# A graph layer on one core: the first dense layer moved into the first gather, windows of 64 columns, and the selection of a turn built by two wide operations

## The reference, cut to what matters

```python
# 12500 nodes of 256 numbers, 212500 edges sorted by dst, all float32
xn = layernorm(x)
def gcn_layer(x, W, b):
    support = x @ W
    return segment_sum(support[src] * edge_weight[:, None], dst) + b
h  = elu(gcn_layer(xn, W1, b1))        # first layer
h  = elu(gcn_layer(h,  W2, b2))        # second layer
x  = x + h + linear_attention_and_mlp(xn)
x  = x + mixture_of_8_experts(layernorm(x))
```

## Time and profile before

| | us |
|---|---|
| median of three runs | 5660.61 |
| span of the profiled execution | 5671.8 |
| POOL busy | 3577.5 (63%) |
| PE busy / its weight loads | 4100.8 (72%) / 3754.5 (66%) |
| DVE busy | 2639.8 (47%) |
| ACT busy | 832.1 (15%) |

### The profile page before, as it was taken

How to read it: one execution, slowest core, us unless ns; L and a number is a source line. 1 busy time by engine, 2 the same in 40 slices (tenths; PEclk the granted TensorE clock), 3 DMA queues, 4 the chain that set the end, 5 groups by cost and what they waited for, 6 DMA issues and landing times. The chain is left out here.

```text
span 5671.8 us, 86295 instructions
## 1 busy us (share of the span) xinstructions
PE 4100.8 (72%) x25350; PEld 3754.5 (66%) x25351; DVE 2639.8 (47%) x8555; ACT 832.1 (15%) x2244; POOL 3577.5 (63%) x3748
## 2 busy tenths in 40 slices
PE   0566666666666666688888888888888777139998
PEld 0466666666656666588778778788787665138887
DVE  7433333333333323755555555555555588324444
ACT  2000000000000000611111111111111144001111
POOL 0677777777777777377777777777777522442222
PEclk9887888888888888899999999999999967569999
DMA  7444444444444444344444444444444366442221
GB/s 219 123 124 124 124 123 124 125 124 124 124 124 124 124 124 114 116 115 118 118 117 118 117 118 117 118 117 118 117 117 117 108 212 209 151 156 70 66 68 64
DMA packets 410309, 699.39 MB, mean 123 GB/s; under 512 B 103966, under 2 KB 276766, under 8 KB 410174
## 3 DMA queue, kind: packets, MB, share of 16 engines
q0 software_dynamic: 177584, 489.12, 30.6%
q1 hardware_dynamic: 196773, 168.65, 9.9%
q10 hardware_dynamic: 35920, 41.25, 2.1%
HBM read 565.09 MB, written 133.62 MB: 123 GB/s over the span
## 5 line engine op out<-in xcount | busy, mean ns | idle before, releaser
L374 PE MATMUL sums<-sel,rows 128*128 128x128 f32 x13312 | 1997.5, 315 | 1037.0 <-DMA rows<-xn,idx 430.3
L374 PEld LDWEIGHTS sums<-sel,rows 128*128 128x128 f32 x13312 | 1910.1, 228 | 1139.0 <-issue 776.3
L421 POOL DMA_INDIRECT rows<-xn,idx x1664 | 1591.3, 956 | 642.5 <-issue 632.8
L421 POOL DMA_INDIRECT rows<-h,idx x1664 | 1590.2, 956 | 529.0 <-issue 511.7
L390 DVE TENSOR_TENSOR agg<-agg,sums 128x256 f32 x416 | 175.6, 422 | 1554.1 <-PE sums L374 1554.1
L384 DVE TENSOR_SCALAR sel<-cols,rel_now,wgt_now 128x128 f32<-128x128 f32 x3344 | 891.4, 364 | 8.0
L1705 PE MATMUL y_ps<-w,e_hidden 128*128 128x256 f32 x1248 | 287.3, 390 | 0.0
L1693 PE MATMUL e_hidden_ps<-tokens_t,w 128*128 128x256 f32 x1248 | 279.9, 382 | 4.9 <-DVE e_hidden L1762 4.0
L1705 PEld LDWEIGHTS y_ps<-w,e_hidden 128*128 128x128 f32 x1248 | 242.8, 197 | 33.6
L1633 POOL DMA_INDIRECT out<-y_result,target_i x80 | 79.8, 998 | 293.5 <-DVE y_result L1747 273.5
L1693 PEld LDWEIGHTS e_hidden_ps<-tokens_t,w 128*128 128x128 f32 x1248 | 237.8, 191 | 40.8 <-DVE e_hidden L1762 7.3
(11 more groups left out here) (205 smaller groups left out, 4874.1 us busy)
## 6 DMA issues: line engine op xcount, KB each, us to landing
xe<-zeros ACTq DMA_DIRECT2D x104, 258.0 KB, 3.8
rows<-xn,idx POOLq DMA_INDIRECT x1664
rows<-h,idx POOLq DMA_INDIRECT x1664
w<-in_ffn_w POOLq DMA_DIRECT2D x16, 1024.0 KB
tile<-xn SPq DMA_DIRECT2D x105, 128.0 KB
ln_rows<-in_x SPq DMA_DIRECT2D x52, 256.0 KB
xn<-ln_normed ACTq DMA_DIRECT2D x52, 256.0 KB, 4.3
kv_tile<-xn SPq DMA_DIRECT2D x104, 128.0 KB
```

What stands on the lines that cost most here:

```text
L374: last = nc.tensor.matmul(sums[g][:, h, :], rows[:, u, k, h * P:(h + 1) * P], sel[:, k, :], start=(c == 0), stop=(c == GROUP - 1))
L421: nc.gpsimd.indirect_dma_start(out=rows[:, u, k, :], out_offset=None, in_=source, in_offset=bass.IndirectOffsetOnAxis(ap=idx[:, u, k:k + 1 ...
```

## The change

Gather stages: a turn keeps its 16 slots but has 4 groups of 4 slots; a window has 64 nodes; two groups share a PSUM bank. `sel` and `rel_now` get two halves. The selection of a whole turn (16 slots by 64 columns, 1024 elements per partition) is built by two tensor-tensor operations one turn ahead, in place of 16 with two per-partition scalars each. PE takes the groups in order; DVE adds four windows, each behind the one before; PE's first product of a turn waits for `turn_added`. The places of the attention's pieces in a turn stay.

First dense layer: units of 128 nodes; the unit of turn t-8 is done in turn t of gather 1 (copy and exp on ACT, product on PE between the two banks, bias, max and elu on DVE, store on SP). After the last turn units 96 and 97 remain. Should a group's first node lie below what was already taken, all units are done again at the end; this is worked out in prepare. The stage of its own is gone, and POOL has no part in the layer. The loops of gather 1 have 6 double turns written out ahead of the loop, where before it was one.

```diff
-GROUP = 8
-TURN = 2
+GROUP = 4
+TURN = 4
+SUB = 2
+BANKS = TURN // SUB
-WIN = 128
+WIN = 64
+LAG = 8
+UNITS = 2 * -(-N // (2 * P))
...
-        def selection(g):
-            for c in range(GROUP):
-                k = g * GROUP + c
-                last = nc.vector.tensor_scalar(sel[:, k, :], m.cols[:, :], rel_now[:, k:k + 1], wgt_now[:, k:k + 1],
-                                               ALU.is_equal, ALU.mult)
-            return last
+        def of_window(of):
+            return of.rearrange("p (c o) -> p c o", o=1).to_broadcast([P, SLOTS, WIN])
+        def same_node(u):
+            return nc.vector.tensor_tensor(sel[:, u, :, :], m.cols[:, :].rearrange("p (o w) -> p o w", o=1)
+                                           .to_broadcast([P, SLOTS, WIN]), of_window(rel_now[:, u, :]), ALU.is_equal)
+        def weigh(u, t):
+            return nc.vector.tensor_tensor(sel[:, u, :, :], sel[:, u, :, :],
+                                           of_window(m.wgt[:, bass.ds(t * SLOTS, SLOTS)]), ALU.mult)
...
                 def turn(i, u):
                     t = 2 * i + u
+                    dense.dve(dve, i, u, 0)
                     mix.dve(dve, i, u, 0)
-                    selection(1).then_inc(sel_ready[1], 1)
+                    if not before_first(i, u, 1):
+                        dve.wait_ge(summed[BANKS - 1], t)
+                    take(t + 1, 1 - u)
                     mix.dve(dve, i, u, 1)
...
-                    add_window(0, low[0]).then_inc(added, 1)
-                    mix.dve(dve, i, u, 2)
...
+                    for g in range(TURN):
+                        if g % SUB == 0:
+                            if g:
+                                mix.dve(dve, i, u, 2)
+                                dense.dve(dve, i, u, 1)
+                            wait_apart(dve, summed[g // SUB], t + 1, m.passed)
+                        if g or not before_first(i, u, 1):
+                            dve.wait_ge(added, t * TURN + g)
+                        add_window(g, low[g]).then_inc(added, 1)
...
-                    take(t + 1)
+                    dve.sem_inc(turn_added, 1)
                     mix.dve(dve, i, u, 3)
...
+    def product(pe, j, u):
+        pe.wait_ge(nodes_ready, 2 * j + (u + 1))
+        for k in range(KD):
+            last = nc.tensor.matmul(z, nodes[:, k, :], w_g1[:, k, :], start=(k == 0), stop=(k == KD - 1))
+    def elu(dve, j, u, fresh):
...
+        nc.vector.tensor_scalar(positive[:, :], pre[:, :], 0.0, -1.0, ALU.max, ALU.add).then_inc(positive_ready, 1)
...
+        nc.vector.scalar_tensor_tensor(h[:, u, :], exps[:, :], 1.0, positive[:, :], ALU.min, ALU.add
+                                       ).then_inc(h_ready, 1)
+    def act(act, i, u, place, turn_added):
+        if due(i, u):
+            if place == 0:
+                act.wait_ge(turn_added, 2 * i + u)
+                copy_nodes(act, i - behind, u, 2 * (i - behind) + u)
+            if place == 1:
+                exponential(act, i - behind, u)
+    def act_end(act, turn_added):
+        act.wait_ge(turn_added, TURNS)
+        for n in range(TURNS - LAG, UNITS):
+            copy_nodes(act, n // 2, n % 2, n)
+            exponential(act, n // 2, n % 2)
...
-            gather(nc, m, 1, m.xn, keys_values)
-            dense_first(nc, m)
-            gather(nc, m, 2, m.h1, attend)
+            gather(nc, m, 1, m.xn, keys_values, dense_first)
+            gather(nc, m, 2, m.h1, attend, apart)
```

More of the change, by code:

```diff
@@ L134, in prepare @@
         span = sb("span", [TURNS, TURN], I32)
-        more = sb("more", [TURNS, 1], I32)
+        more = sb("more", [TURNS, 2], I32)
+        least = sb("least", [TURNS, 1], I32)
+        taken = sb("taken", [TURNS, 1], I32)
         dst_i = sb("dst_i", [P, NCH], I32)
@@ L263, in _ @@
                 dve.wait_ge(step, 4)
-                nc.vector.tensor_reduce(more[:, :], high[:, :], AX.X, ALU.max).then_inc(spans_done, 1)
-                stat_steps = 5
+                nc.vector.tensor_reduce(more[:, 0:1], high[:, :], AX.X, ALU.max).then_inc(step, 1)
+                nc.vector.tensor_reduce(least[:, :], low[:, :], AX.X, ALU.min).then_inc(step, 1)
+                wait_apart(dve, taken_ready, 1, m.passed)
+                dve.wait_ge(step, 6)
+                nc.vector.tensor_tensor(more[:, 1:2], least[:, :], taken[:, :], ALU.is_lt).then_inc(spans_done, 1)
+                stat_steps = 7
                 def statistics(i, s):
@@ L365, in gather, with window_products @@
         further_step = sem("further_step")
+        further_steps = 2 + TURN
         mix = mixer(nc, m, sb, sem, ps)
+        dense = denser(nc, m, sb, sem, ps)
         loops = TURNS // 2
-        def window_products(g, h, u, before):
-            for c in range(GROUP):
-                k = g * GROUP + c
[L374 to L377, removed]
-            return last
-        def selection(g):
-            for c in range(GROUP):
-                k = g * GROUP + c
-                last = nc.vector.tensor_scalar(sel[:, k, :], m.cols[:, :], rel_now[:, k:k + 1], wgt_now[:, k:k + 1],
-                                               ALU.is_equal, ALU.mult)
-            return last
+        def window_products(b, s, u, before):
+            for h in range(KD):
+                for c in range(GROUP):
+                    k = (b * SUB + s) * GROUP + c
+                    last = nc.tensor.matmul(sums[b][:, s, h, :], rows[:, u, k, h * P:(h + 1) * P], sel[:, u, k, :],
+                                            start=(c == 0), stop=(c == GROUP - 1))
+                    if h == 0 and c == 0 and before is not None:
+                        last.then_inc(before, 1)
+            return last
+        def of_window(of):
[6 more added lines that the diff above has]
+                                           of_window(m.wgt[:, bass.ds(t * SLOTS, SLOTS)]), ALU.mult)
         def add_window(g, at):
             window = m.agg[:, :, bass.ds(at, WIN)]
-            return nc.vector.tensor_tensor(window, window, sums[g][:, :, :], ALU.add)
+            return nc.vector.tensor_tensor(window, window, sums[g // SUB][:, g % SUB, :, :], ALU.add)
         with nc.Block(f"gather{layer}") as block:
@@ L398, in _, with turn @@
                 mix.load_weights(sp)
-                with sp.Fori(1, loops) as i:
-                    for u in range(2):
[L402 to L407, removed]
+                dense.load_weights(sp)
+                def turn(i, u):
+                    sp.wait_ge(rows_loaded[u][BANKS - 1], 16 * GROUP * SUB * i)
+                    sp.dma_start(idx[:, u, :], m.in_src[bass.ds(2 * i + u, 1)].rearrange("o p c -> (o p) c")
+                                 ).then_inc(idx_loaded[u], 16)
+                    mix.free(sp, i - 1, u)
+                    mix.load(sp, 2 * i + u, u)
+                    mix.store(sp, i - 1, u)
+                    dense.sp(sp, i - 1, u)
+                for i in range(1, dense.peeled):
+                    for u in range(2):
+                        turn(i, u)
+                with sp.Fori(dense.peeled, loops) as i:
+                    for u in range(2):
+                        turn(i, u)
+                for u in range(2):
+                    dense.sp(sp, loops - 1, u)
                 mix.load_past(sp)
                 mix.stored(sp)
+                dense.sp_end(sp)
                 sp.wait_ge(m.xe_zeroed, 16 * TURNS)
@@ L516, in _, with apart @@
-                two_by_two(pe, loops, turn)
+                    mix.pe(pe, i, u, TURN)
+                two_by_two(pe, loops, turn, dense.peeled)
                 mix.pe_end(pe)
+                dense.pe_end(pe)
         mix.after()
+def apart(nc, m, sb, sem, ps):
+    dense = Memory()
+    dense.peeled = 1
+    dense.load_weights = dense.sp_end = dense.dve_begin = dense.dve_end = lambda engine: None
+    dense.pe_end = dense.pe_begin = lambda engine: None
+    dense.sp = dense.pe = lambda engine, i, u: None
+    dense.dve = lambda engine, i, u, place: None
+    dense.act = lambda engine, i, u, place, turn_added: None
+    dense.act_end = lambda engine, turn_added: None
+    return dense
```

341 lines of the change are left out of this document (187 added, 154 removed).

## The result

The changed kernel takes 5682.15 us (median of 5 runs, 5681.56 to 5695.59), the kernel before 5663.88 us beside it (5 runs, 5658.44 to 5666.25). The ratio is 1.0038, with a 95% interval of 1.0025 to 1.0051: slower, by 18 us in the medians. The profiled execution took 5681.56 us.

A forecast was written before the change was run, and what follows sets the result against it. POOL's indirect DMA strings were taken to bound the kernel. The removed stage's -90 us and +95 us, mainly from wide operations stopping POOL, gave +5 on the 5660.6 us median: 5666 us, range 5620 to 5715 (8 in 10: 5590 to 5745).

The forecast's parts named there:

- The bound: Both gathers: POOL's unbroken strings of 1664 indirect DMAs set the time, 20.2 us a turn; PE and DVE keep pace.
- The stage between the gathers: Between POOL's two strings: 122.4 us without row fetches shrinks, gaining 93 us, taken as 90.
- The 3 us taken off: Off the stage's gain: first products wait for both wide operations (2.5 us); gather 2's last products may run at lower clock.
- The first wide operation: Selection in both gathers: stops POOL's DMA until it ends, 0.46 us a turn in the mean at equal chance.
- The Trainium skill's rule taken whole: Shared SBUF port: a two-SBUF-input operation holds POOL for all 1.23 us; 0.60 us a turn, some 25 us slower than forecast.
- The second wide operation: Selection in both gathers: ends 1.26 us after the first, adding 0.03 us a turn to POOL's stops.
- The old selection's share: Both gathers: the removed narrow selection's part in POOL's longer DMAs, 10 us back.
- The min-and-add: Elu of the dense layer moved under POOL: two SBUF inputs also stop POOL, 3 us.
- Narrower windows: PE's window products: 64 columns take the same time as 128, nothing gained, nothing lost.
- Wide operations that seldom stop POOL: Rival, both gathers: wide operations cost POOL only 0 to 0.15 us a turn; about 5580 us; chance 0.13.
- A stop of nearly the whole length: Rival, each turn of both gathers: wide operations stop POOL 1.0 us a turn, 208 us; 5771 us; chance 0.09.
- PE as the bound: Rival, gather 1: low clock makes PE's turn 21.6 us against 20.2, 150 us more; 5768 us; chance 0.08.

The follow-up runs named there:

- E1: Changed kernel with the two wide selection operations replaced by 16 narrow ones a turn: 5571.61 us, ratio 0.9828 to the kernel before.
- E3: Changed kernel with a third wide operation right behind the two in gather 2, into a spare tile: 5689.84 us, ratio 1.0031 to the kernel before.
- E7: Changed kernel with a third wide operation by itself in gather 2, between the adds of the two banks: 5727.06 us, ratio 1.0118.
- E2: Changed kernel with node numbers and weights copied to PSUM in gather 1 alone, wide operations kept, gather 2 as control: 5635.08 us, ratio 0.9937.
- E5: Narrow windows alone: changed kernel with 16 narrow selection operations and the dense layer back between the gathers: 5654.20 us, ratio 0.9986.
- E6: Changed kernel with each wide operation cut into 8 pieces in gather 1 and 4 in gather 2: 5598.62 us, ratio 0.9892.

## Why the prediction came out as it did

**The bound** was right: POOL's string sets both gathers before and after, and E1 shows that all else that moved fits under it.

**The stage between the gathers**: -91.8 us where the steps gave -93, less 3. The steps hold one by one: the last bank's products began 3.6 us after POOL's last DMA (forecast 3.7), the two units took 3.3 us each (forecast 3.5). The gap came to 30.6 us where the steps gave 29.1. The 3 us taken off rested in part on the wrong reason. E1 and E3 both have a shorter gap, 26.2 and 27.1 us, and E3 keeps the wide operations. What differs is PE's clock at the end: the changed kernel's 16 last products, then E1's and E3's:

```profile
2320.56 3.52 PE L380 MATMUL sums<-sel,rows 128*128 128x64 f32 x16
```
```profile
2260.46 1.90 PE L380 MATMUL sums<-sel,rows 128*128 128x64 f32 x16
2321.53 1.90 PE L381 MATMUL sums<-sel,rows 128*128 128x64 f32 x16
```

The granted clock over the last 32 products of gather 1's windows was 0.52 in the changed kernel's profile, 1.00 in E1's and E3's. The forecast had priced the low clock, and in this profile it was granted; at the high one the gap would have been some 3 us shorter.

**The first wide operation**: 98.1 us over 208 turns, 0.47 each, where equal chance gave 0.46. The mechanism held, but that the size came so close was partly luck. The moments aren't spread evenly: of the 201 in L390, 56 lie 0.30 to 0.45 us into it and none in the next 0.15. And the first operation's loss in a single gather 2 went from 0.35 us a turn (E7) over 0.40 (E3) to 0.54 (E2). What sets the place against POOL's beat stays open. The unheld first 0.15 us, taken from two rows, held in all 27 cases. The Trainium skill's rule taken whole (SBUF — State Buffer, "Who interferes with whom") made it 0.60; E2 bears out its condition, two SBUF inputs, and the trace its length only without that start.

**The second wide operation** is the term that was mis-sized: 0.03 us a turn expected, 0.084 measured, 17.4 us in place of 6. I had its end follow the first's by 1.26 us; it waits for the first's result and starts 1.35 us after it, 0.09 behind POOL's beat of 1.255.

**The old selection's share** was put at 10 us, read as 11.1. **The min-and-add** was put at 3, read as 2.1. **Narrower windows** were put at nothing. For the time that held as far as E5 tells; the 9 us less stretch there lie in narrow operations of selection, which the changed kernel doesn't have. For PE it didn't hold: its clock fell.

**Sum.** -91.8 + 98.1 + 17.4 - 11.1 + 2.1 = +14.7, for +5 forecast; 11 of the difference are the second operation. The medians differ by 18 us, the two profiled spans by 8. The profile before was taken of an execution whose span lay 11 us over the median, the changed kernel's of one within 2 us of it. The undisturbed DMA took 949 ns in the first and 946 in the second, 10 us over 3328, and such a step also shows between E1 (946) and E2 (949) on one chip. No run tells where it comes from.

**The rivals.** Wide operations that seldom stop POOL would have given means of 0.95 to 0.96; they were 0.99. A stop of nearly the whole length would have been 1.0 us a turn; it was 0.55. PE as the bound: its first half came true, the clock fell in gather 1, to 0.74 (and to 0.67 in E5), but POOL waited only 1.8 us for PE there.

## What to carry to other kernels

When one engine's string sets the time, ask of each new operation on another engine not how long it is but what it reads: here two SBUF operands on VectorE held up the indirect DMAs whose moment fell inside, past the operation's first 0.15 us. One operand in PSUM (E2) took that away, and scalars by pointer (E1) nearly did. A gain and a loss of the same size hide each other in the total; the loss of 0.4% here was a 1.7% gain (E1) with its price on top. Many short operations can beat two long ones when a neighbour has to slip between them.

## What the hardware showed that I had not expected

The place of an operation decided more than the number: the same 1.2 us cost nothing behind two others and 47 us over 104 turns by themselves (E3, E7). Operations without a wait between them overlap: eight pieces of 286 ns passed in 1.71 us (E6). And the stop goes both ways: a DMA whose moment came just ahead made the operation wait, 11 times in the changed kernel, while in E2's gather 1 no operation took over 1.222 us.
